# W_x's products with 96 columns as weights and 512 tokens streaming, in the four rotating banks

## The reference, cut to what matters

```python
proj = hidden_states @ W_in.T
x, gate = (proj[..., :D_IN], proj[..., D_IN:])        # D_IN = 2048
...                                                    # causal convolution of 4 taps
x = jax.nn.silu(xc)
ssm = x @ W_x.T                                        # 96 = R + 2 N, R = 64, N = 16
ts, Bm, Cm = (ssm[..., :R], ssm[..., R:R + N], ssm[..., R + N:])
ts = rms_forward(ts)
Bm = rms_forward(Bm)
Cm = rms_forward(Cm)
dt = jax.nn.softplus(ts @ W_dt.T + b_dt)
def step(state, inp):
    dA = jnp.exp(dt_t[..., None] * A)
    state = state * dA + (dt_t * u_t)[..., None] * B_t[:, None, :]
    y = jnp.einsum('bdn,bn->bd', state, C_t)
```

## Time and profile before

| | us |
|---|---|
| median of 3 runs | 2970.67 (2968.34 to 2972.52) |
| the profiled execution's own time | 2971.96 |
| its span, first to last instruction | 2969.9 |
| PE busy | 2729.3 |
| DVE busy | 2552.7 |
| POOL busy | 1922.2 |
| ACT busy | 1695.5 |
| granted TensorE clock, mean | 0.968 of full speed |

### The profile page before, as it was taken

One profiled execution on the slowest core, in us unless ns is written; L12 is line 12 of the kernel. 1 busy time (PEld: TensorE's weight loads), 2 busy tenths in 40 slices (PEclk: granted clock), 3 DMA queues, 4 the chain that ended last, 5 costly groups with the idle time before them and its releaser, 6 DMA issues.

```text
span 2969.9 us, 35293 instructions
## 1 busy us (share of the span) xinstructions
PE 2729.3 (92%) x11120; PEld 1557.2 (52%) x11120; DVE 2552.7 (86%) x3525; ACT 1695.5 (57%) x2848; POOL 1922.2 (65%) x886
## 2 busy tenths in 40 slices
PE   8988899999989999998999887888889999999996
PEld 4444555555555555555555454555544555555553
DVE  2289999999999999999999999999966787787785
ACT  2366556565665657566565654756534555555553
POOL 1179798888969889896988988889731222222221
PEclk9998999999999999999999999889899999999998
DMA  5352333433343343334333333322401211111110
GB/s 173 132 123 72 112 104 95 136 116 110 91 152 105 94 135 120 107 99 144 110 93 97 100 87 94 121 87 65 113 29 38 97 56 56 64 56 56 64 60 26
DMA packets 132876, 281.32 MB, mean 95 GB/s; under 512 B 12528, under 2 KB 12656, under 8 KB 132224
## 3 DMA queue, kind: packets, MB, share of 16 engines
q1 hardware_dynamic: 132736, 279.59, 31.1%
HBM read 245.86 MB, written 33.69 MB: 94 GB/s over the span
## 4 chain that ended last, share of the span: by engine, by line
PE 54%; DVE 32%; issue 8%; ACT 4%; POOL 1%; DMA 0%; DVEq 0%; POOLq 0%; SPq 0%; ACTq 0%
DVE arena L1429 17%; PE banks L524 16%; PE banks L548 9%; DVE arena L1445 7%; PE banks L618 7%; PE banks L764 4%; PE banks L717 4%; PE banks L673 3%; PE banks L698 3%; PE banks L561 2%; PE banks L688 2%; PE banks L728 2%; ACT banks L1166 1%; DVE arena L1376 1%; PE banks L771 1%
## 5 line engine op out<-in xcount | busy, mean ns | idle before, releaser
L1344 POOL TENSOR_TENSOR arena<-arena 128x2048 f32<-128x2048 f32 x255 | 1158.6, 4544 | 78.5 <-PE banks L618 78.5
L1429 DVE TENSOR_TENSOR_SCAN arena<-banks,arena 128x512 f32<-128x512 f32 x1024 | 1184.7, 1202 | 14.9 <-POOL arena L1344 8.9
L1166 ACT ACTIVATE banks<-arena,a_sb 128x508 f32<-128x508 f32 x1024 | 696.8, 684 | 727.9 <-DVE arena L1429 724.2
L524 PE MATMUL banks<-arena 128*128 128x512 f32 x2048 | 954.6, 603 | 11.4 <-DMA arena<-in_xT 8.2
L618 PEld LDWEIGHTS banks<-ident,arena 128*128 128x128 f32 x4096 | 490.4, 145 | 396.7 <-issue 177.4
L618 PE MATMUL banks<-ident,arena 128*128 128x128 f32 x4096 | 572.5, 283 | 115.1 <-DVE arena L1445 64.1
L524 PEld LDWEIGHTS banks<-arena 128*128 128x128 f32 x2048 | 373.0, 195 | 363.1 <-issue 358.8
L1445 DVE SCALAR_TENSOR_TENSOR arena<-banks,cg,arena 128x512 f32<-128x512 f32 x640 | 452.4, 737 | 76.4 <-PE banks L618 75.8
L548 PE MATMUL banks<-arena 128*128 128x512 f32 x1024 | 472.9, 601 | 5.7 <-DMA arena<-in_WoutT 4.4
L1276 POOL TENSOR_TENSOR arena<-arena 128x512 f32<-128x512 f32 x240 | 306.9, 1279 | 207.2 <-ACT arena L910 204.8
L1357 POOL TENSOR_TENSOR arena<-arena 128x512 f32<-128x512 f32 x128 | 141.4, 1104 | 431.9 <-DVE arena L1610 431.8
(11 more groups left out here) (139 smaller groups left out, 2973.3 us busy)
## 6 DMA issues: line engine op xcount, KB each, us to landing
arena<-b_scratch SPq DMA_DIRECT2D x128, 512.0 KB, 5.1
arena<-in_WinX SPq DMA_DIRECT2D x128, 256.0 KB, 2.8
arena<-in_WinZ SPq DMA_DIRECT2D x128, 256.0 KB, 2.7
arena<-in_WoutT SPq DMA_DIRECT2D x32, 1024.0 KB, 5.9
u_scratch<-arena SPq DMA_DIRECT2D x64, 256.0 KB, 5.1
arena<-u_scratch SPq DMA_DIRECT2D x16, 1024.0 KB, 9.5
arena<-x_scratch SPq DMA_DIRECT2D x32, 512.0 KB, 3.4
arena<-in_xT SPq DMA_DIRECT2D x14, 1024.0 KB, 8.2
```

Source lines behind the costliest of these rows:

```text
L524: last = nc.tensor.matmul(home(kind, i), wr[w % 2][:, k, :], x[:, k, :], start=(k == 0), stop=(k == KC - 1))
L1166: nc.scalar.activation(by_seq(bank(i % 2))[:, :, 1:SEQ], by_seq(dt[s % 2][:, i, :])[:, :, 1:SEQ], ACT.Exp, scale=a_sb[:, QD * q + i, n:n + ...
L1344: nc.gpsimd.tensor_tensor(hb[n % 4].rearrange("p (i t) -> p i t", i=QD), dtu, brep[pair % 3][:, n % 2:n % 2 + 1, :].broadcast_to([P, QD, G ...
L1429: nc.vector.tensor_tensor_scan(h, bank(i % 2), h, 0.0, ALU.mult, ALU.add)\
```

## The change

1. `S` becomes a kind of job: pair p has a place in `JOBS` and so one of banks 4 to 7. It is listed in `ORDER` and `OPENING` with 0 filler steps, since `pe_ssm` still issues it by hand at the same iterations. `FREED` for it is `ss_added`.
2. `pe_ssm` takes the 96 columns of `wxT` as weights and streams 512 tokens: two products instead of eight. The waits for `acc_ok` before it, and for `ss_added` before the next turn 0, go.
3. The sums lie by channel: `ssacc` is 96x512. `dve_ss_add` works on 96x512 instead of 128x384.
4. Once per group `pe_ss_turn` turns `ssacc` in four transposes into the last pair's bank. ACT squares from there and copies the sums to the new `ssx`, from which `act_ss_norm` reads. In the steps that end a group the turn lies in iteration 2 behind turn 1, and the square moves from slot e = 17 to e = 18.
5. `part2` shrinks to one buffer, to make room: `act_part2` waits for POOL's sum before.
6. In step 0 the convolution of X tile 20 comes earlier: its base in slot 26 instead of 27, its taps in iteration 4 instead of 5.

```diff
-OPENING = "X-2 X-1 Z0 X0 D0 Z1 X1 D1 D2 Z2 D3 X2 Z3 X3".split()
-ORDER = ["Z0 X0 Z1 D0 X1 D1 Z2 D2 O0 O1 O2 O3 D3 X2 Z3 X3 O4 O5 O6 O7".split()] * (NQ - 1) + \
-    ["Z0 X0 O0 O1 O2 O3 D0 Z1 D1 X1 D2 Z2 D3 X2 Z3 X3 O4 O5 O6 O7".split()]
+OPENING = "X-2 X-1 S-1 Z0 X0 D0 S0 Z1 X1 D1 D2 Z2 D3 X2 S1 Z3 X3".split()
+ORDER = ["Z0 S0 X0 Z1 D0 X1 D1 Z2 D2 O0 O1 O2 O3 D3 X2 S1 Z3 X3 O4 O5 O6 O7".split()] * (NQ - 1) + \
+    ["Z0 S0 X0 O0 O1 O2 O3 D0 Z1 D1 X1 D2 Z2 D3 X2 S1 Z3 X3 O4 O5 O6 O7".split()]
...
         def pe_ssm(pe, p):
+            pe_room(pe, "S", p)
             pe.wait_ge(S["u_ok"], 2 * p + 2)
-            after(pe, "ss_added", p)
...
-            for b in range(GB):
-                for m in (2 * p, 2 * p + 1):
-                    last = nc.tensor.matmul(bank(2)[:, b * SS:(b + 1) * SS], cv[m % 3][:, b * P:(b + 1) * P],
-                                            wxT[:, m % DT, :], start=(m == 2 * p), stop=(m == 2 * p + 1))
+            for m in (2 * p, 2 * p + 1):
+                last = nc.tensor.matmul(home("S", p)[0:SS, :], wxT[:, m % DT, :], cv[m % 3],
+                                        start=(m == 2 * p), stop=(m == 2 * p + 1))
             last.then_inc(S["ss_mm"], 1)
+        def pe_ss_turn(pe, g):
+            pe.wait_ge(S["ss_added"], DT // 2 * (g + 1))
+            for b in range(GB):
+                last = nc.tensor.transpose(home("S", DT // 2 * (g + 1) - 1)[:, b * SS:(b + 1) * SS],
+                                           ssacc[0:SS, b * P:(b + 1) * P], ident[0:SS, 0:SS])
+            last.then_inc(S["ss_turned"], 1)
...
-                if n == 2 and has_x(s - 1):
-                    pe.wait_ge(S["ss_added"], (LEAD + QD * s) // 2)
...
-                if n == 12 and has_x(s):
-                    pe.wait_ge(S["ss_added"], (LEAD + QD * s) // 2 + 1)
                 turn(0)
                 turn(1)
+                if n == 2 and q == NQ - 1 and s + 1 < NS:
+                    pe_ss_turn(pe, g + 1)
...
                 if n == 1 and has_x(s - 1):
-                    pe.wait_ge(S["acc_ok"], kept(s, n, SPLIT))
                     pe_ssm(pe, (LEAD + QD * s) // 2 - 1)
...
         def act_ss_square(act, g):
-            act.wait_ge(S["ss_added"], DT // 2 * (g + 1))
+            act.wait_ge(S["ss_turned"], g + 1)
...
-            nc.scalar.activation(ssn, ssacc, ACT.Square).then_inc(S["ss_square"], 1)
+            nc.scalar.activation(ssn, turned, ACT.Square).then_inc(S["ss_square"], 1)
+            after(act, "ss_normed", 3 * GB * g)
+            nc.scalar.activation(ssx, turned, ACT.Copy).then_inc(S["ss_copied"], 1)
...
-            v = ssacc.rearrange("p b s -> p (b s)")
+            v, new = ssacc[0:SS, :], home("S", p)[0:SS, :]
...
-            if s == 0 and n in (0, 3, 5, 7):
-                dve_taps(dve, X - 2 + (0, 3, 5, 7).index(n))
+            if s == 0 and n in (0, 3, 4, 7):
+                dve_taps(dve, X - 2 + (0, 3, 4, 7).index(n))
```

More of the change, by code:

```diff
@@ L88, in job @@
         return ("X", LEAD + QD * s + i) if has_x(s) else None
+    if kind == "S":
+        return ("S", (LEAD + QD * s) // 2 + i - 1) if has_x(s if i else s - 1) or s == 0 else None
     if kind == "O":
@@ L106, in jobs @@
 def jobs():
-    found = [("X", m) for m in range(EARLY - 1)] + [("D", i) for i in range(QD)] + [("X", EARLY - 1)]
+    found = []
+    for m in range(EARLY - 1):
+        found += [("X", m)] + ([("S", (m - 3) // 2)] if m % 2 == 1 and m >= 3 else [])
+    found += [("S", DT // 2 - 1)] + [("D", i) for i in range(QD)] + [("X", EARLY - 1)]
     for s in range(NS):
@@ L160, in program @@
         brep = [at(1024 * i, 2, GT) for i in range(3)]
-        part2 = at(3072, 2, QD * P)
+        part2 = at(3072, QD * P)
+        ssacc = at(3584, GT)
         hb = [at(4096 + 2048 * i, QD * GT) for i in range(4)]
@@ L178, in program @@
         wxT = at(44544, DT, SS)
-        ssacc = at(46080, GB, SS)
+        ssx = at(46080, GB, SS)
         ssn = at(46464, GB, SS)
@@ L510, in pe_room @@
                 kind, i = JOBS[k - 4]
-                pe.wait_ge(S[FREED[kind]], i + 1)
+                if kind == "S" and (i + 1) % (DT // 2) == 0:
+                    pe.wait_ge(S["ss_copied"], (i + 1) // (DT // 2))
+                else:
+                    pe.wait_ge(S[FREED[kind]], i + 1)
         def pe_tile(pe, kind, i, k):
@@ L878, in act_ss_norm @@
             act.wait_ge(S["ss_rstd"], g + 1)
+            act.wait_ge(S["ss_copied"], g + 1)
             for b in range(GB):
-                nc.scalar.activation(ssn[:, b, lo:hi], ssacc[:, b, lo:hi], ACT.Copy, scale=ss3[:, j, b:b + 1])\
+                nc.scalar.activation(ssn[:, b, lo:hi], ssx[:, b, lo:hi], ACT.Copy, scale=ss3[:, j, b:b + 1])\
                     .then_inc(S["ss_normed"], 1)
@@ L921, in act_part2 @@
             else:
-                after(act, "sum2_ok", (len(SHARED) - 1) * s + k - 2)
-                dst = part2[:, k % 2, :]
+                after(act, "sum2_ok", (len(SHARED) - 1) * s + k - 1)
+                dst = part2
             nc.scalar.activation(dst, bank(2), ACT.Identity, scale=cg[:, SPLIT, n:n + 1])\
@@ L960, in act_opening @@
                 act_x_sig(act, X - 1)
-            if e == 27:
+            if e == 26:
                 act_base(act, X)
@@ L1028, in act_between @@
             if e == 17:
-                if q == NQ - 1 and more:
-                    act_ss_square(act, g + 1)
                 act_z_exp(act, Z)
@@ L1034, in act_between @@
                 act_z_sig(act, Z)
+                if q == NQ - 1 and more:
+                    act_ss_square(act, g + 1)
             if mine and e == 20:
@@ L1283, in pool_sums2 @@
             after(pool, "sum2_ok", (len(SHARED) - 1) * s + k - 1)
-            nc.gpsimd.tensor_tensor(acc2, acc2, part2[:, k % 2, :], ALU.add).then_inc(S["sum2_ok"], 1)
+            nc.gpsimd.tensor_tensor(acc2, acc2, part2, ALU.add).then_inc(S["sum2_ok"], 1)
         def pool_u(pool, m):
@@ L1381, in dve_ss_add @@
         def dve_ss_add(dve, p):
-            v = ssacc.rearrange("p b s -> p (b s)")
+            v, new = ssacc[0:SS, :], home("S", p)[0:SS, :]
             dve.wait_ge(S["ss_mm"], p + 1)
             if p % (DT // 2) == 0:
-                last = nc.vector.tensor_copy(v, bank(2)[:, 0:GB * SS])
+                after(dve, "ss_turned", p // (DT // 2))
+                last = nc.vector.tensor_copy(v, new)
             else:
                 dve.wait_ge(S["ss_added"], p)
-                last = nc.vector.tensor_tensor(v, v, bank(2)[:, 0:GB * SS], ALU.add)
+                last = nc.vector.tensor_tensor(v, v, new, ALU.add)
             last.then_inc(S["ss_added"], 1)
@@ L1781, in _ @@
             pe.wait_ge(S["pool_const"], 1)
-            pe.wait_ge(S["ss_added"], DT // 2)
+            pe_ss_turn(pe, 0)
             pe_rows(pe, 0)
```

11 lines of the change are left out of this document (5 added, 6 removed).

## The result

| | before | after |
|---|---|---|
| median, us | 2971.30 (4 runs, 2968.34 to 2972.52) | 2944.36 (4 runs, 2942.54 to 2945.36) |
| the profiled execution's own time | 2971.96 | 2944.21 |
| its span | 2969.9 | 2942.2 |
| granted TensorE clock, mean | 0.968 | 0.971 |

The change makes the kernel faster: the ratio is 0.991, 95% interval 0.9893 to 0.9927, that is 26.9 us by the medians. The prediction was 2941 us, with 29.5 us saved.

The account below looks back on a forecast made before the run. PE and DVE, both nearly full, were taken to bound the steady step by turns. Savings of 31.6 + 3.1 - 2.0 - 1.2 - 2.0 = 29.5 us took 2971.96 to 2942.5, as median 2941 us; whole range 2933 to 2958.

Parts of the forecast that it names:

- PE's wait: PE's idle time for DVE before the `W_x` products, on 24 pairs inside the recurrence: all 31.6 us would go.
- Rival B: PE stands at its next turn, the bank or `u_ok` instead of the products; 31.6 us stay, 2971 us; chance 0.06.
- C (the ring): Filler meets an unread bank among the four, holding up turns and scans; 4.1 us per step, 2986 us; chance 0.05.
- The pair: Two `W_x` products on PE take 1.74 us against 1.87: 0.13 us less, 24 times, 3.1 us.
- Iteration 1: Steady step: PE's next turn comes 1.49 us earlier, and DVE's gap lets 1.47 us through.
- Iteration 11: Steady step: PE is 1.38 us earlier, and all of it passes through DVE's three gaps by iteration 14.
- Rival A: DVE keeps half: gains in mid-step only lengthen its later waits; 13 us saved, 2957 us; chance 0.11.
- Step 0 and the first steps: Step 0 and group-ending steps have partly shorter waits and a nearer DVE cap: 2.0 us off, bounds 0 and 6.
- Behind the layer norm's statistics: Steps 5 and 9: PE's second wait, 2.23 us, goes, the first stays; no better clock booked, up to 5 us possible.
- The turn once per group: Prologue 1.2 us slower; in steps 3, 7 and 11 PE 0.5 us each, ACT 0.2 at most, together 2.0 us.
- X tile 20's taps: Step 0: taps an iteration earlier, some 8 us, cover X tile 21; without it PE would stand 2.1 us once.

Follow-up runs that it names:

- experiment 1: The banks alone against the kernel before: products in their old form in the change's rotating banks, without the waits, no turn; 2939.64 us, ratio 0.9888.
- experiment 2: The change with the wait for `acc_ok` put back in front of the products inside the steps; 2971.96 us, ratio 0.9997 to the kernel before.
- Experiment 7: The change with POOL's product of a step's last z tile moved to the next step's iteration 3, behind the sum of state 15; 2936.55 us.
- experiment 3: The change with POOL's second sum of state 12 one iteration later; 2948.62 us, and 2948.23 us when run again.
- experiment 4: The kernel before with POOL's second sum of state 12 one iteration later; 2972.68 us, ratio 0.9998.
- Experiment 10: The kernel before with POOL's product of the last z tile moved behind the sum of state 15; 2964.50 us, ratio 0.9976.
- experiment 5: The change with X tile 20's convolution in step 0 back in slot 27 and its taps in iteration 5; 2949.18 us, ratio 0.9923.

## Why the prediction was right, and where it was not

The direction, the mechanism and the size hold: 26.9 us saved against 29.5, the size in part by luck. Its steps one by one:

**PE's wait, right.** All 31.6 us go, nothing waits in their place at the banks or at `u_ok`, and experiments 1 and 2 show that this wait, taken away by the banks, is the gain. Rival B (the wait moves on) is ruled out by DVE's idle time, and C (the ring) by the steps, none of which got longer.

**The pair, right and idle.** 1.72 us instead of 1.74, 0.15 less than before. It buys nothing that can be measured: experiment 1 keeps the old pair and is as fast. By the isolated gap of N/2.4 + 2.5 ns in the Trainium skill ("TensorE: Matmul & The Clock Gate", section "Back-to-back issue gap"), with two passes per instruction, the estimate is 1.73 us for the new pair and 1.36 us for the old. The trace agrees with the first (1.72 us) and not with the second: the old pair took 1.87 us.

**Iteration 1, right.** Forecast 1.47 us; the scans come 1.56 us earlier than the step's offset in step 2 (2.85 against 1.29 at the turns of iterations 0 and 1).

**Iteration 11, the step that failed.** It was said that POOL and ACT are asked 2.85 us sooner per step "and have 16 us or more". PE's turns do come 1.2 us earlier there, but the step keeps less than 0.5 of it. POOL's 16 us are real: 4.70 us at one wait, 3.43 and 3.37 at others, nearly all of them in the first half of the step. In the second half POOL has next to none. I had read its room as an average over the step, and not over the stretch between the place of the gain and the place where the step ends. Had I listed POOL's waits in that stretch, the trace of before would have shown a single spare 0.42 us in 66 us, beside 0.17 us between two instructions of its own, and a steady step of 126.36 - 1.56 - 0.42 = 124.38; measured 124.33. Experiment 7 shows the cause, as it gives the missing 0.8 us back, and experiment 3 that the order inside the queue is not it. Against the forecast of 2.85 this lost 0.82 us in each of six steady steps, 5.0 us. Rival A, that not all of iteration 11 comes through, is closer for these steps, but for another reason: DVE had room, POOL had none.

**Step 0 and the first steps, worse than booked.** Three pairs there had idle time that went, and the step kept 0.09 us of it. PE's turns are 2.2 us earlier in iteration 13, but POOL is 0.6 us late, since it waited 4.69 us for ACT up to 255.60, where it waited 3.51 us up to 255.02 before, and the step ends with POOL. PE also stands 3.26 us for a D tile in both kernels. How much of it is POOL and how much the clock was not separated.

**Behind the layer norm's statistics, better than booked.** PE before:

```profile
842.84 1.04 PE L618 MATMUL banks<-ident,arena 128*128 128x128 f32 x8
```

```profile
836.79:842.84 6.05, 6.04 (x20) 4.58 (x21) 2.75 (x3) 3.58 (x7) 5.34 (x2) 0.58 0.00 0
842.84:853.00 10.16, 10.16 (x48) 6.18 (x47) 9.52 (x11) 5.63 (x8) 5.85 (x5) 1.00 0.36 110
```

and after:

```profile
824.89 1.64 PE L634 MATMUL banks<-ident,arena 128*128 128x128 f32 x8 [2.79 <-DVE arena L1459]
826.32 3.29 PE L569 MATMUL banks<-arena 128*96 128x512 f32 x4
829.45 1.88 PE L533 MATMUL banks<-arena 128*128 128x512 f32 x4
```

```profile
826.32:829.45 3.13, 3.13 (x6) 1.18 (x6) 3.13 (x5) 1.98 (x3) 0.31 (x1) 0.55 0.00 1
829.45:840.00 10.55, 10.55 (x44) 6.09 (x43) 9.95 (x13) 7.91 (x13) 9.58 (x6) 1.00 0.39 96
```

The pair still runs at the lower clock (0.55 granted), 3.13 us against 1.72, but the second wait of 2.23 us is gone, and the filler behind the pair has a granted clock of 1.00: 1.71 us from its start to the next turn, where it took 842.84 - 840.32 = 2.52.

Counted from the start of the step, PE is back at full speed 5.7 us sooner (24.40 us before, 18.70 after). The Trainium skill ("TensorE: Matmul & The Clock Gate", section "The HAM clock gate") says that idleness lowers the clock. The direction agrees: one wait went and the other fell from 3.46 to 2.79 us. In the profiles of the kernels that have the wait at the products (before, experiments 2, 4 and 10) steps 5 and 9 take 134.6 to 136.5 us, in those without it 130.3 to 132.4. How much of that is the clock varies: step 5 had its clock at the lower level for 6.8 us before, 3.4 us after, not at all in experiment 1 and for 6.8 us in experiment 7.

Steps 5 and 9 gave 4.44 and 4.88 us, 2.4 and 2.9 more than a steady step. This is what the forecast named as possible and did not book. It and the 3.1 us in steps 12 to 14, of which the forecast had none, make up for the loss at POOL. That the total came so near is in part luck. Steps 12 to 14 have no products of `W_x`, and with the wait put back (experiment 2) they take 360.5 us, with the kernel before and one sum of POOL moved (experiment 4) 361.0, against 363.9 before and 360.8 after: their 3.1 us are not the wait's. Experiment 10 shortens two of them by POOL alone, so they are sensitive to POOL, but what shortened them in the change was not traced.

**The turn once per group, right.** In the prologue 0.82 us were lost against 1.2 forecast. In step 3 the change's scan of iteration 5 is 0.80 us later after the step's start than with the banks alone, where the sum of 0.5 and 0.2 was forecast; three times that is 2.1 us, and 2.0 was booked. That the turn itself waits for DVE's addition, 2.4 us in all (L577), was not foreseen.

**X tile 20's taps**: the cover was needed as said; without it the price is 3.7 us in step 0, and not 2.1 us.

## What to carry to other kernels

Room on an engine is read between the place where a gain arises and the place where it has to arrive: list that engine's waits in that stretch and take the sum, never the busy share of the whole step. An engine that is busy 87% of a step can be full for the half that matters, and then the little spare time in that half caps the gain. If it does, move work of that engine to behind the instruction that others wait for; moving it about ahead of that instruction gave nothing here, even where it cleared a wait that the profile showed. And where a change alters both the form of a piece of work and what it waits for, run the two apart: here the banks alone, with the old form, were as fast as the whole change.

## What was not expected of the hardware

A stretch of 4.0 us in which PE stood (experiment 5) was followed by 5.3 us at a granted clock of 0.50, in which PE did what takes 2.6 us elsewhere. The wait cost more than its own length. And behind the layer norm's statistics, with one of two waits gone and the other shorter, PE was back at full speed right after the pair: the stretch from the turn's start to full speed took 4.56 us after, and 9.59 us before (833.25 to 842.84). Even the remaining wait of 2.79 us (the turn at 824.89) was followed by a stretch at 0.55. The time at the lower level also differed between kernels that both lack the wait at the products (3.4 us in step 5 of the change, 6.8 us in experiment 7). Like schedules differed by up to 3 us in the steps that have such waits, while the steady steps, with the granted clock at 1.00, repeated to 0.1 us.
